# Tensor product of a graph network: features turned by half packs at two places of a turn, flags copied first, index loads one turn ahead

## What is computed

```python
R = relu(edge_weight[:, None] @ w1 + b1) @ w2 + b2        # 400000 x 384 radial weights
Y = spherical_harmonics(edge_attr_3)                      # direction of each edge
Fj = h[src]                                               # 32 features of the source node: 8 scalars, 8 vectors
for i, (mo, lo) in enumerate(RS):                         # RS = [(8, 0), (8, 1)]
    for j, (mi, li) in enumerate(RS):
        for k, lf in enumerate(range(abs(lo - li), lo + li + 1)):
            acc += norm[i] * einsum('euv,ef,evi,ofi->euo', R[..., k], Y[lf], F[j], C[lo, lf, li])
out = zeros.at[dst].add(concatenate(msg))                 # edges are sorted by dst
```

## Time and profile before

| | us |
|---|---|
| median of 3 runs | 8630.15 (8627.51 to 8634.26) |
| the profiled execution | 8642.33 |
| its span, first to last instruction | 8640.3 |
| of it: gathers of the tensor product, first to last | 4409.2 to 8466.1 |
| DVE busy over the span | 5311.7 (61%) |
| POOL busy over the span | 6479.9 (75%) |
| PE busy over the span | 3594.6 (42%) |
| granted PE clock, mean | 0.721 of full speed |

### The profile page before, as it was taken

One profiled execution on the slowest core, in us unless ns is written; L12 is line 12 of the kernel. 1 busy time (PEld: TensorE's weight loads), 2 busy tenths in 40 slices (PEclk: granted clock), 3 DMA queues, 4 the chain that ended last, 5 costly groups with the idle time before them and its releaser, 6 DMA issues. The chain is left out here.

```text
span 8640.3 us, 61009 instructions
## 1 busy us (share of the span) xinstructions
PE 3594.6 (42%) x15884; PEld 2458.9 (28%) x15884; DVE 5311.7 (61%) x7917; ACT 1921.1 (22%) x2576; POOL 6479.9 (75%) x6677
## 2 busy tenths in 40 slices
PE   1000000000000000000048888888888888888882
PEld 0000000000000000000035655556555656655651
DVE  3233333343333433334369999999999999999993
ACT  0123332223322233222201111111111111111110
POOL 7777777777777777777667777777777777777775
PEclk6555555555555555555579999999999999999996
DMA  7333444334443444443222222222222222222221
GB/s 301 102 107 109 116 113 122 107 109 114 113 124 107 110 112 114 122 111 110 63 52 70 68 66 67 69 68 66 67 70 68 66 68 70 66 68 66 70 66 29
DMA packets 364374, 796.10 MB, mean 92 GB/s; under 512 B 143582, under 2 KB 209998, under 8 KB 344638
## 3 DMA queue, kind: packets, MB, share of 16 engines
q1 hardware_dynamic: 99880, 491.45, 19.3%
q0 software_dynamic: 213216, 166.16, 10.3%
q10 hardware_dynamic: 51126, 136.22, 4.2%
HBM read 499.72 MB, written 293.61 MB: 92 GB/s over the span
## 5 line engine op out<-in xcount | busy, mean ns | idle before, releaser
L993 POOL DMA_INDIRECT feat<-scratch_h,src x3132 | 3102.2, 990 | 975.1 <-issue 954.7
L537 POOL DMA_INDIRECT kv<-scratch_kv,src_i x3132 | 2971.9, 949 | 959.8 <-issue 959.8
L1020 PE MATMUL psS<-prod,ident 128*128 128x288 f32 x7656 | 1986.2, 417 | 0.7 <-ACT red L1082 0.7
L1241 DVE TENSOR_TENSOR prod<-psR,ops 128x384 f32<-128x384 f32 (+1 forms) x3132 | 1919.6, 682 | 82.7 <-PE psR L1009 47.3
L804 PE MATMUL psA<-ident,tail 128*36 128x128 f32 x3 | 0.8, 413 | 3936.5 <-DVEq L829 3936.5
L1020 PEld LDWEIGHTS psS<-prod,ident 128*128 128x128 f32 x7656 | 1505.0, 198 | 423.4 <-issue 14.1
L1008 PE MATMUL psR<-whigh,stack 128*128 128x384 f16 x3132 | 1066.8, 341 | 540.7 <-DVE prod L1241 531.1
L804 PEld LDWEIGHTS psA<-ident,tail 128*36 128x36 f32 x3 | 0.3, 127 | 3936.7 <-DVEq L829 3936.6
L1009 PE MATMUL psR<-wlow,capped 128*128 128x384 f16 x3132 | 1067.7, 342 | 0.0
L689 DVE TENSOR_TENSOR qk<-psQ,kv 128x1728 f32<-128x1728 f32 x58 | 113.6, 1958 | 1473.7 <-DMA kv<-scratch_kv,src_i 1473.7
L1082 ACT ACTIVATE red<-psS,scales 128x288 f32<-128x288 f32 x348 | 174.6, 502 | 2388.7 <-PE psS L1023 2388.3
(11 more groups left out here) (254 smaller groups left out, 4039.3 us busy)
## 6 DMA issues: line engine op xcount, KB each, us to landing
w_row<-in_wT SPq DMA_DIRECT2D x116, 864.0 KB
stack<-scratch_hid SPq DMA_DIRECT2D x174, 576.0 KB
scratch_state<-out ACTq DMA_DIRECT2D x58, 1080.0 KB
kv<-scratch_kv,src_i POOLq DMA_INDIRECT x3132
qin<-scratch_qexp SPq DMA_DIRECT2D x58, 864.0 KB, 4.5
scratch_hid<-high SPq DMA_DIRECT2D x116, 432.0 KB, 11.1
scratch_hid<-low SPq DMA_DIRECT2D x116, 432.0 KB, 12.0
feat<-scratch_h,src POOLq DMA_INDIRECT x3132
```

The lines of the kernel that those rows point to most:

```text
L537: nc.gpsimd.indirect_dma_start(kv[b][:, t, :], None, a["kv"], bass.IndirectOffsetOnAxis(ap=src_i[b][:, t:t + 1].bitcast(U32), axis=0)).the ...
L993: nc.gpsimd.indirect_dma_start(feat[h][:, t, :], None, a["h2"], bass.IndirectOffsetOnAxis(ap=src_i[b][:, h * PACK + t:h * PACK + t + 1].bi ...
L1020: nc.tensor.matmul(into, ident[:, :], prod[r][:, :, j, :], start=(n == 0), stop=False)
L1241: v.tensor_tensor(to[:, :, :, lo:lo + n], psR[:, g % 2, :, frm:frm + n * JC].rearrange("p t (j u) -> p t j u", j=JC), ops[j % 2][:, ts, x ...
```

## The change

Five edits, all in `tensor_product`:

1. `rotate` and `operands` work on half a pack (9 slots) and are called twice a turn for pack j + 1: half 0 after the first fold, half 1 where the whole pack stood before. `scalars` and `turned` on ACT are split likewise, half 0 between `store` and the eviction of half 0, half 1 where they stood.
2. `feat_free` is counted by halves, and POOL waits for it ahead of each 9 gathers; each half of a buffer has its own arrival semaphore.
3. The copy of the flags (`same_c`) moves on ACT from the end of `seeds` to the front of `frames`; DVE waits for it ahead of rotating half 0.
4. The index load of ACT moves from the last turn of a chunk to the one before it (`j % PACKS == PACKS - 2`).
5. The waits of `products` on `turned_ready` and `turned_copied` stand at both halves.

Nothing changes on PE. The diff's core:

```diff
+HALVES = 2
+HALF_PACK = PACK // HALVES
...
                         for h in range(PACKS):
-                            pool.wait_ge(feat_free, i * TURN + b * PACKS + h + 1)
-                            pool.sem_inc(pack_begun, 1)
-                            for t in range(PACK):
+                            for x in range(HALVES):
+                                pool.wait_ge(feat_free, i * (TURN * HALVES) + (b * PACKS + h) * HALVES + x + 1)
+                                pool.sem_inc(half_begun, 1)
+                                for t in range(x * HALF_PACK, (x + 1) * HALF_PACK):
...
                     for n, at, wanted in ((0, j - 1, begun), (1, j + 1, more)):
                         if wanted:
+                            if n == 0:
+                                back_at = at % PACKS * PACK + 1
+                                nc.scalar.activation(same_c[:, :, 1:P1], spread_front(
+                                    k["same"][:, bass.ds(i * 2 + at // PACKS, 1), back_at:back_at + PACK].rearrange("p c t -> p (c t)"), VU),
+                                    ACT.Copy).then_inc(flags_ready, 1)
...
                             store(i, j - 2)
+                        if more:
+                            scalars(i, j + 1, 0)
+                            turned(i, j + 1, 0)
                         for s in range(SPP - 1):
                             evict(i, j, s)
                         if more:
-                            scalars(i, j + 1)
-                        if j % PACKS == PACKS - 1 and not last:
+                            scalars(i, j + 1, 1)
+                        if j % PACKS == PACKS - 2 and not last:
                             b = j // PACKS
                             act.dma_start(src_i[b][:, :], sources[:, bass.ds(i * (2 * T) + (b + 2) * T, T)]).then_inc(src_loaded[b], 16)
                         if more:
-                            turned(i, j + 1)
+                            turned(i, j + 1, 1)
...
-                    for n in range(3):
-                        step(v.tensor_tensor(parts[:, :, n, :].rearrange("p t (i u) -> p t i u", i=3),
-                                             f[:, :, VU:D].rearrange("p t (i u) -> p t i u", i=3),
+                        step(v.tensor_tensor(parts[:, ts, n, :].rearrange("p t (i u) -> p t i u", i=3),
+                                             f[:, ts, VU:D].rearrange("p t (i u) -> p t i u", i=3),
...
-                    if s == 0:
-                        vec.wait_ge(turned_ready, i * TURN + j + 1)
+                    vec.wait_ge(turned_ready, i * (TURN * HALVES) + j * HALVES + s + 1)
...
                         products(i, j, 0, first)
                         fold(i, j, 0)
+                        if begun:
+                            vec.wait_ge(flags_ready, i * TURN + j)
+                        if more:
+                            rotate(step, i, j + 1, 0)
+                            operands(step, i, j + 1, 0)
                         products(i, j, 1, first)
                         fold(i, j, 1)
...
                         if more:
-                            rotate(step, i, j + 1)
-                            operands(step, i, j + 1)
+                            rotate(step, i, j + 1, 1)
+                            operands(step, i, j + 1, 1)
```

More of the change, by code:

```diff
@@ L928, in tensor_product @@
         src_loaded, frame_here, stacked = ([sem(f"{n}{b}") for b in range(2)] for n in ("src_loaded4", "frame_here", "stacked"))
-        feat_here = [sem(f"feat_here{h}") for h in range(PACKS)]
+        feat_here = [[sem(f"feat_here{h}_{x}") for x in range(HALVES)] for h in range(PACKS)]
         feat_free, frame_free, stored = sem("feat_free"), sem("frame_free4"), sem("stored4")
@@ L934, in tensor_product @@
             "ops_copied", "turned_ready", "turned_copied", "ops_free", "flags_ready4", "red_free", "scanned", "run_copied"))
-        seeded, vec_done, pack_begun = sem("seeded"), sem("vec_done4"), sem("pack_begun")
+        seeded, vec_done, half_begun = sem("seeded"), sem("vec_done4"), sem("half_begun")
         frames_ready = sem("frames_ready4")
@@ L1104, in _ @@
                 act.wait_ge(frame_here[0], 16)
-                scalars(0, 0)
-                turned(0, 0)
+                for x in range(HALVES):
+                    scalars(0, 0, x)
+                    turned(0, 0, x)
                 def body(i, first, last):
@@ L1137, in _ @@
                 v = nc.vector
-                for primed, n in ((feat_free, PACKS), (prod_done, 6), (sum_free, 2), (ops_free, 2),
+                for primed, n in ((feat_free, PACKS * HALVES), (prod_done, 6), (sum_free, 2), (ops_free, 2),
                                   (red_free, 2), (scanned, 1), (run_copied, 1)):
@@ L1199, in _, with rotate @@
                 vec.sem_inc(scales_steps, 1)
-                def rotate(step, i, j, at=None):
+                def rotate(step, i, j, x, at=None):
                     f = feat[j % PACKS]
+                    ts = slice(x * HALF_PACK, (x + 1) * HALF_PACK)
                     if at is None:
@@ L1238, in products @@
                             x = max(0, lo // VU - 1)
-                            if s == 0 and third == 0 and x == 1:
-                                vec.wait_ge(turned_copied, i * (TURN * 2) + j * 2 + 2)
+                            if third == 0 and x == 1:
+                                vec.wait_ge(turned_copied, i * (TURN * 2 * HALVES) + j * (2 * HALVES) + 2 * s + 2)
                             v.tensor_tensor(to[:, :, :, lo:lo + n], psR[:, g % 2, :, frm:frm + n * JC].rearrange("p t (j u) -> p t j u", j=JC),
@@ L1281, in _ @@
                 vec.wait_ge(frame_here[0], 16)
-                rotate(step, 0, 0, frame[0][:, 0:PACK, :])
-                operands(step, 0, 0)
-                base, per_pack, of_finish = step.count[0], 11, 6
+                for x in range(HALVES):
+                    rotate(step, 0, 0, x, frame[0][:, 0:PACK, :])
+                    operands(step, 0, 0, x)
+                base, per_pack, of_finish = step.count[0], 16, 6
                 def body(i, first, last):
```

33 lines of the change are left out of this document (16 added, 17 removed).

## The result

The changed kernel takes 9177.11 us (median of 4 runs, 9173.49 to 9179.0) against 8631.71 for the kernel before: ratio 1.0629, with the interval 1.0615 to 1.0642. It is 545 us slower. The forecast was 9079 with a range up to 9170, so the direction held and the size was 98 us too small, 7 us outside the range. The profiled execution took 9173.49, its span is 9171.7 and its mean granted clock 0.698.

What follows compares the result with a forecast made beforehand. Gathers bound the kernel at 23.31 us a turn; the PE-DVE ring would take over: 22.04 + 2.27 (half step) + 1.6 (clock) = 25.9, over 172 turns plus 4 us of edges 9079 us, range 8930 to 9170.

Steps and rivals of the forecast that it cites:

- The ring as the new bound: PE and DVE waiting on each other: 22.04 us a turn becomes 24.31, above the gathers' 23.31.
- What would show it: Signs: fold-to-g3 gap 2.3 us; PE idle 4, clock 0.93 or less; feature wait gone, psR wait 3; POOL idle 2.5.
- ACT, the flags, the index load, the buffers by halves: The change's other parts: hidden or free, with 1.8 us to spare for ACT's scalars.
- The clock's term: PE's pause ahead of radial g5 grows to 4.0 us; one half-clock passage a turn adds 1.6 us, bounds 0 and twice 1.68.
- the rival of two in a row: PE's low clock lasts two 3.4 us stretches, costing up to 2.5 us: turn 26.8, 9235 us; chance 0.09.
- all passages I saw ended once PE was busy: Argument on PE's clock, given against low clock lasting through two stretches of 3.4 us.
- The half step: Half 0 of rotate and operands on DVE between fold and product g3: 2.27 us in series, bounds 1.9 and 2.5.
- The sum: Tensor product: 172 turns x (25.9 - 23.31) = 445 us, plus 4 us for the stage's edges, giving 9079 us.
- The range: Whole kernel: 8930 (today's clock drops) to 9170 (half step's upper bound and part of two passages).
- now it mostly falls into slack: Kernel before: PE's clock passages, 1.9 us a turn, about one every second turn, mostly hidden.
- The "faster" rival: Gathers stay the bound and lose stalls beside DVE's fold: turn 22.5, 8492 us; chance 0.04.

Runs made afterwards that it cites:

- e3: The change with twelve idle matmuls on PE in the pause ahead of radial g5: 8809.92 us, ratio 1.0197 to the kernel before.
- e1: The change with half 0 of rotate and operands moved behind product g3: 8615.63 us, ratio 0.9973 to the kernel before.
- e4: The change with both halves of rotate and operands at the end of the turn, on DVE and ACT: 8633.5 us, ratio 0.9994.
- e5: The kernel before with only the flags' copy at the front of frames and the index load one turn earlier: 8632.54 us, ratio 1.0.
- e8: The kernel before with only six idle matmuls added on PE ahead of radial g5: 8575.08 us, ratio 0.9935.
- e14: The kernel before with four idle matmuls on PE ahead of radial g4: 8576.7 us, ratio 0.9932.
- e13: The kernel before with six idle matmuls ahead of radial g5 and DVE's loop written out: 8552.44 us, ratio 0.9909.
- e2: The change with radial g5 behind the sums of half 0 on PE instead of ahead of them: 8897.23 us, ratio 1.0298.
- e11: The change with four idle matmuls on PE between radial g4 and radial g5: 9102.67 us, ratio 1.0548.
- e12: The change with half 0 behind product g3 and six idle matmuls, DVE's loop kept: 8566.1 us, ratio 0.9917 to the kernel before.

## Why the prediction was right in direction and short in size

Right, step by step:

- *The ring as the new bound.* 22.04 us plus the half step was forecast at 24.31 at full clock; e3 shows 24.16. e1 shows that the place alone does it.
- *What would show it.* All four signs came: the gap between fold and g3 (2.11 us for 2.3), PE idle 3.86 us for "about 4", a clock of 0.89 for "0.93 or less", DVE's wait for features gone and that for psR at 3.5 us a turn for 3. POOL idles 3.7 us a turn where 2.5 was said, as the turn is longer than forecast.
- *ACT, the flags, the index load, the buffers by halves*: free, by e4 and e5, and by the wait of `operands` for the scalars, 7.7 us in the whole stretch of the change.

Mis-sized, in the order of their weight:

- **The clock's term: "one passage in each turn, wholly in the ring, at 1.6 us".** One passage in each turn was right; its length was not. Three in four are two stretches long. Over the stage's turns radial g5 to the sums of half 0 takes 1.89 us on average instead of 0.99, and from there to radial g0 7.69 instead of 6.30: 2.29 us, 0.7 more than forecast. 172 turns by 0.7 are 120 us too little. A single passage cost less than forecast, 1.34 us for 1.6, so all of the shortfall lies with the double ones at 2.61. The step that failed is the argument against the rival of two in a row, "all passages I saw ended once PE was busy": I had only seen passages behind pauses of 1.74 us, and the pause that I forecast was more than twice as long. The rows did not bear the argument out either: in the low stretch of the earlier trace rows PE is busy for all of its 3.40 us. The second low stretch in the rows above lies over a PE that is busy throughout. The rival's turn of 26.8 us (9235) was nearer to the 26.43 measured than mine of 25.9, and I gave it 9 in 100.
- *The half step*: 2.27 forecast, 2.11 measured. `rotate` came out as priced (599 ns before, 368 now, 1.07 ns an element), but the three reductions fell by 0.75 us, from 1.76 to 1.01, where the product's line gave 0.68, and the rest lies between the instructions. That is 28 us too much, and by luck gives part of the error back.
- *The sum*: 24.16 + 2.29 = 26.45 for a turn, against 25.9; 172 x 0.55 = 95 us, and 9079 + 95 = 9174 against 9177.
- *The range.* Its top took in only "part of two passages". It should have gone at least to the rival's 9235; the upper bound that the text itself gave for the clock's term, twice 1.68, would make it about 9384.

Wrong beside the forecast: **"now it mostly falls into slack"**, on the 72 passages of the kernel before. e8 and e14 show that they cost 57 us. DVE's waits for PE are indeed small there, but the passages still lengthen the gathers, which are the bound. In the turns of before (from product g0 to product g0) with a passage the gathers' surplus over 0.95 us is 0.99 us together, in those without 0.60; in e8 it is 0.48. How a late PE leads to more gathers beside DVE's fold is not shown here, only that it does.

The "faster" rival had its mechanism right: gathers can lose their stalls, 60 to 84 us of the 146 that there are (3102.2 us less 3132 times the 0.944 of an undisturbed one), by a clock that stays up (e8, e13) and, 65 us of them, by half steps that stand behind g3 (e1). It did not come about in the change, where the gathers' busy time is 3101.6 us and POOL is no longer the bound.

## What to carry to other kernels

Ahead of inserting work on one engine, find the ring of waits between the engines and its slack (here 1.3 us); work of 2.1 us inside it made it 2.1 us longer and with that the bound, by 0.9 us a turn at full clock and over 3 with the clock that it lost, and behind the next three products it cost nothing. When such an insertion lengthens a pause of PE, price the clock with more than the passage seen so far: a pause of 3.9 us brought two low stretches where one of 1.7 had brought one. A few idle matmuls in PE's pauses, into columns that nobody reads, are a cheap test of what the clock costs, also in a kernel where PE is not the bound.

## What the runs showed of the hardware

- The granted clock can stay low over a second stretch in which PE is fully busy. This was the more frequent the longer the pause before it: 96 of 128 passages lasted 6.8 us at a pause of 3.86, 31 of 131 at 2.97, none of 72 at 1.74. In e2, 6 of 72 did, and each of the six began in a pause of 4.5 to 4.8 us at the head of DVE's loop.
- Four idle matmuls (1.05 us) a turn of 23 us ahead of radial g4 held the clock at 1.00, though a pause of 1.67 us remained (e14); six ahead of radial g5 did too (e8). With the pauses of the change four did not (0.92), twelve did (1.00).
- Of a gather and a two-operand sum in SBUF the one that started first went ahead: in all the traces a gather begun more than 0.1 us into a fold ended 0.81 us or more behind the fold, one begun 0.1 us or more ahead of it kept its 0.94 to 0.96 us.
- A DVE loop body of 351 instructions jumps back without a pause (before, e5). One of 429 or 432 pauses 2.3 to 2.6 us at the head (e4; the change, e1, e2, e3, e11, e12), and the instruction queue of the page goes from 27 packets to 159 or 160. Where between the two sizes it begins was not tried.

```profile
q14 instruction: 27, 0.22, 0.0%
```
```profile
q14 instruction: 159, 1.30, 0.0%
```

These two lines are from the pages of before and of the change: queue and kind, packets, MB, share of the 16 DMA engines.
